# Attention kernel on one core: the part ahead of the loop rebuilt (order of the loads, place of the weight split, banks of the first row maxima)

## What is computed

```
x = x + block(group_norm(x))                   # x: 8 images, 512 channels, 32x32 = 1024 tokens
block(v):
    p    = sigmoid(relu(mean(v) @ w1 + b1) @ w2 + b2)        # gate: one value per channel
    m    = p > 0.5
    hyp  = logmap0(mhsa(expmap0(v * m), hdn weights))        # norms along the 32 pixels of a row
    euc  = mhsa(v * (1 - m), eu weights)
    return hyp + euc
mhsa: q,k,v = split(t @ w_qkv + b_qkv); 8 heads of 64; softmax(q k^T / 8) v; then @ w_o + b_o
```

## Time and profile before

| | us |
|---|---|
| median of 3 runs (4372.26 to 4374.09) | 4373.63 |
| the profiled execution | 4372.58 |
| span of its instructions | 4370.9 |
| of it ahead of the first score of the loop | 209.4 |

### The profile page before, as it was taken

The page is one execution under the profiler, slowest core; times in us unless marked ns, Lnnn a source line. Parts: engine busy times, 40 slices in busy tenths (PEclk is TensorE's granted clock), DMA queues, the critical chain, the costliest instruction groups (busy, mean ns, idle before and its releaser), DMA issues.

```text
span 4370.9 us, 69097 instructions
## 1 busy us (share of the span) xinstructions
PE 4039.6 (92%) x21822; PEld 2426.7 (56%) x21822; DVE 2652.2 (61%) x2771; ACT 1933.8 (44%) x3504; POOL 2668.0 (61%) x1303
## 2 busy tenths in 40 slices
PE   0599989999999989999899998999989998999989
PEld 0355646565465655656465564656546565565645
DVE  4446684557736676465854658455773667646585
ACT  0145453544535445354534545355452544535453
POOL 0167376755758458584676737676575845858467
PEclk9899999999999999999999999999999999999999
DMA  7211212112131211212121121211203121121212
GB/s 273 87 37 49 95 43 95 54 71 73 34 105 44 80 54 56 88 51 87 54 96 41 45 99 39 98 54 61 82 32 108 44 80 54 54 91 51 87 52 83
DMA packets 147413, 314.94 MB, mean 72 GB/s; under 512 B 17600, under 2 KB 30400, under 8 KB 136512
## 3 DMA queue, kind: packets, MB, share of 16 engines
q1 hardware_dynamic: 147008, 309.92, 20.7%
HBM read 259.54 MB, written 50.33 MB: 71 GB/s over the span
## 4 chain that ended last, share of the span: by engine, by line
PE 82%; DVE 9%; issue 4%; DMA 3%; ACT 1%; SPq 0%; DVEq 0%; POOL 0%; ACTq 0%
PE aux_ps L1035 29%; PE acc_ps L1137 20%; PE score_ps L1123 19%; PE aux_ps L1076 8%; PE score_ps L1035 3%; DVE mxp L944 3%; PE aux_ps L1147 2%; DMA xin<-in_x_dram 1%; DMA w_split<-o_t 1%; DVE sc L812 1%; PE aux_ps L1085 1%; DVE sc L819 1%; DVE sc L820 0%; DVE den L972 0%; DVE xin L905 0%
## 5 line engine op out<-in xcount | busy, mean ns | idle before, releaser
L588 POOL TENSOR_TENSOR sums<-sums,probs 128x1024 f32<-128x1024 f32 x768 | 1867.4, 2432 | 892.5 <-ACT probs L714 852.2
L944 DVE TENSOR_REDUCE mxp<-aux_ps 128x2 f32<-128x1024 f32 x1041 | 1274.0, 1224 | 1218.5 <-PE aux_ps L1076 1205.1
L714 ACT ACTIVATE probs<-score_ps 128x512 f32<-128x512 f32 x2048 | 1056.9, 602 | 663.9 <-PE score_ps L1123 656.0
L1137 PE MATMUL acc_ps<-probs,v_y 128*64 128x512 f32 x4096 | 1017.6, 618 | 0.0
L1035 PE MATMUL aux_ps<-xs,w_qk 128*128 128x512 f32 x3168 | 871.0, 414 | 40.8 <-DMA w_qk<-w_split 40.8
L1035 PEld LDWEIGHTS aux_ps<-xs,w_qk 128*128 128x128 f32 x3168 | 572.4, 192 | 465.0 <-issue 301.7
L588 POOL TENSOR_TENSOR sums<-probs 128x1024 f32<-128x1024 f32 x128 | 305.2, 2384 | 538.4 <-ACT probs L714 538.4
L1076 PE MATMUL aux_ps<-k_hi,q_hi 64*128 64x512 f32 x2082 | 481.2, 456 | 159.0 <-DVE mxp L944 153.1
L1137 PEld LDWEIGHTS acc_ps<-probs,v_y 128*64 128x64 f32 x4096 | 251.6, 138 | 477.4 <-issue 438.6
L972 DVE RECIPROCAL den<-den 128x256 f32<-128x256 f32 (+1 forms) x240 | 443.9, 1849 | 7.7 <-ACT den L725 7.7
L1123 PE MATMUL score_ps<-q_hi,k_hi 64*128 64x512 f32 x2048 | 408.8, 395 | 20.6 <-issue 20.6
(11 more groups left out here) (114 smaller groups left out, 3377.9 us busy)
## 6 DMA issues: line engine op xcount, KB each, us to landing
xin<-in_x_dram SPq DMA_DIRECT2D x280, 256.0 KB, 2.9
w_qk<-w_split SPq DMA_DIRECT2D x134, 512.0 KB, 4.1
w_v<-w_split SPq DMA_DIRECT2D x34, 1024.0 KB, 6.8
w_o<-w_split SPq DMA_DIRECT2D x32, 1024.0 KB, 7.1
w_split<-o_t SPq DMA_DIRECT2D x16, 1024.0 KB, 5.5
y<-v_y SPq DMA_DIRECT2D x64, 256.0 KB, 2.0
v_y<-in_x_dram SPq DMA_DIRECT2D x64, 256.0 KB, 2.8
xin<-y SPq DMA_DIRECT2D x64, 256.0 KB, 2.7
```

Of the source, the lines that this page charges most:

```text
L588: pool.tensor_tensor(sums[h][:, :], a, probs[:, g % SLOTS_P, :], ALU.add).then_inc(c_sum[h].sem, 1)
L714: act.activation(probs[:, n % SLOTS_P, token_half(u % 2)], score_ps[:, u % SCORE_BANKS, :], ACT.Exp, scale=SCALE).then_inc(c_exp.sem, 1)
L944: dve.tensor_reduce(mxp[:, :, n, h], ps, AX.X, ALU.max).then_inc(c_free["D"].sem, 1)
L1137: last = nc.tensor.matmul(acc_ps[head(j), :], v_y[:, m, head(2 * p + j)], probs[:, n % SLOTS_P, token_half(j)], start=(m == 0), stop=(m == ...
```

## The change

All of it lies ahead of the loop, apart from waits in the loop for things made there.

- **x once and first.** The 8 chunks of image 0 are loaded once, as SP's first transfers, into the eight parts of `v_y`. Statistics, squares (written to `o_raw`, `squares` and `den`), masks and the operand all work from there. Gate weights and gate biases come next, then six raw weight pieces, then the other biases.
- **The weight split on ACT and POOL.** `split_hi` (ACT, 128x1024 copy) and `split_lo` (POOL, 128x1024 subtraction) replace the two DVE instructions. There are six raw slots (`probs` and `sums`) and ten places for the result (`o_t`, `w_v`, `w_o`, `v_y`). ACT makes three high parts ahead of its two instructions in the gate, three behind them, and the other ten between its read-outs of projection tiles (`SPLIT_BEHIND`). POOL makes three low parts once the gate is done and the other thirteen once the operand is complete. After each low part SP loads the next raw piece and stores the finished one, as before, 16 stores in all.
- **In place.** The projections of pairs 0 and 1 read their weights from the first two split places in `o_t`, and the loop's first v tiles from `w_v`, without a trip to DRAM.
- **The operand's low parts** of image 0 are made by DVE (`x_lo`), between its multiplications.
- **The first row maxima** take three pairs of banks in turn (0 and 1, and the four score banks), the projection tiles bank 2 and the accumulator's bank. The order (`AHEAD`) is: two projection tiles, four maxima, a tile, four maxima, a tile, then four times two maxima and a tile of pair 1.
- In the loop ACT waits for `weights_lo_made` ahead of the first four exponentials of an image and for two stores ahead of its v read-outs; both are met for good once the split is over.

```
+SPLIT_SLOTS = [0, 1, 6, 7, 2, 3, 4, 5, 8, 9, 2, 3, 4, 5, 0, 9]
+SPLIT_FIRST = 6
+SPLIT_BEHIND = {(PAIRS, 0): (6, 7), (PAIRS, 1): (8, 9), (PAIRS, 2): (10, 11), (PAIRS, 3): (12, 13),
+                (PAIRS + 1, 0): (14,), (PAIRS + 1, 1): (15,)}
+LOW_FIRST = 3
+AHEAD = [("qk", PAIRS, 0), ("qk", PAIRS, 1), *[("max", PAIRS, s) for s in range(4)],
+         ("qk", PAIRS, 2), *[("max", PAIRS, s) for s in range(4, 8)], ("qk", PAIRS, 3)]
+for k in range(4):
+    AHEAD += [("max", PAIRS, 8 + 2 * k), ("max", PAIRS, 9 + 2 * k), ("qk", PAIRS + 1, k)]
 def aux_tiles(t):
 
...
-                out += maxima(p, s)
-            out += [((t, "qk", p + 1, k), "Q", (2,))]
+        for what, pp, k in AHEAD:
+            if what == "qk":
+                out += [((t, what, pp, k), "Q", ((2, ACC)[k % 2],))]
+            else:
+                first = (0, FIRST_SCORE, FIRST_SCORE + 2)[k % 3]
+                out += [((t, what, pp, k), "D", (first, first + 1))]
         return out + neg(p) + maxima(p + 1, 0)
     out = []
     for b in range(BATCHES):
...
-        for c, parts in enumerate(SRCS):
-            count[c % 3] += 16 * len(parts)
-            raw_at.append(count[c % 3])
+        raw_at = [16 * sum(len(SRCS[SPLITS[m]]) for m in range(n % RAW_SLOTS, n + 1, RAW_SLOTS)) for n in range(len(SPLITS))]
+        def raw_slot(n):
+            q = n % RAW_SLOTS
+            return probs[:, q, :] if q < SLOTS_P else sums[q - SLOTS_P][:, :]
+        def split_slot(n):
+            q = SPLIT_SLOTS[n]
+            if q < 4:
+                return o_t[:, q // 2, 2 * (q % 2):2 * (q % 2) + 2, :]
+            if q < 8:
+                w = (w_o, w_v)[q // 2 - 2]
+                return w[:, q % 2, :, :, :].rearrange("p a k n -> p a (k n)")
+            return v_y[:, 4 * (q % 2):4 * (q % 2) + 4, :].rearrange("p (a k) n -> p a (k n)", a=2).bitcast(F32R)
 
         def token_half(h):
...
 
         def xin_slot(t, kind, j):
+            if t < 0 and kind == "norm":
+                return (o_raw[:, 0, :], o_raw[:, 1, :], squares[:, :], den[:, 1, :])[j % 4]
+            if t < 0 and kind != "w":
+                return v_y[:, j, :]
             return xin[:, chunk_at(t, kind, j) % XIN, :]
 
         def chunk_in(eng, i, t, kind, j):
 
+            if t < 0 and kind != "w":
+                eng.wait_ge(c_x[j].sem, c_x[j].at(i, 16))
+                return v_y[:, j, :]
...
-                sp.dma_start(bias_o[:, t, :], bo.rearrange("(k p) -> p k", p=P)).then_inc(s_bias, 16)
-            sp.dma_start(bias_1[:, :], b1.rearrange("(p a) -> p a", a=1)).then_inc(s_bias, 16)
-            sp.dma_start(bias_2[:, :], b2.rearrange("(k p) -> p k", p=P)).then_inc(s_bias, 16)
-            def store_split(c):
-                sp.wait_ge(s_split, 2 * c + 2)
-                sp.dma_start(w_split[c], o_t[:, c % 2, 0:2, :].rearrange("p a n -> p (a n)").bitcast(F32)).then_inc(s_wst[c % 2], 16)
...
+            def load_raw(n):
+                raw = raw_slot(n)
+                for src, j in SRCS[SPLITS[n]]:
...
+                    sp.dma_start(dst, src).then_inc(s_raw[n % RAW_SLOTS], 16)
...
-            load_chunks(None, -1, "stats", range(8))
+            for j in range(8):
+                k, cols = x_chunk(j)
+                sp.dma_start(v_y[:, j, :], x_v[0, k, :, cols]).then_inc(c_x[j].sem, 16)
             load_gate(None, -1)
-            load_chunks(None, -1, "norm", range(8))
-            load_chunks(None, -1, "operand", range(8))
+            sp.dma_start(bias_1[:, :], b1.rearrange("(p a) -> p a", a=1)).then_inc(s_gate_bias, 16)
+            sp.dma_start(bias_2[:, :], b2.rearrange("(k p) -> p k", p=P)).then_inc(s_gate_bias, 16)
+            for n in range(RAW_SLOTS):
+                load_raw(n)
+            for t, (bq, bo) in enumerate(((hb_qkv, hb_o), (eb_qkv, eb_o))):
+                for j in range(3):
+                    sp.dma_start(bias_q[:, t, j, :], bq[j * C:(j + 1) * C].rearrange("(k p) -> p k", p=P)).then_inc(s_bias, 16)
+                sp.dma_start(bias_o[:, t, :], bo.rearrange("(k p) -> p k", p=P)).then_inc(s_bias, 16)
+            for n, c in enumerate(SPLITS):
+                sp.wait_ge(s_wlo, n + 1)
+                if n + RAW_SLOTS < len(SPLITS):
+                    load_raw(n + RAW_SLOTS)
+                sp.dma_start(w_split[c].rearrange("p (a n) -> p a n", a=2), split_slot(n).bitcast(F32)).then_inc(s_wst[n], 16)
             for q in s_wst:
-                sp.wait_ge(q, 16 * 8)
+                sp.wait_ge(q, 16)
             i = None
             for j in range(2):
-                load_qk(-1, PAIRS, j)
-            load_wide(w_v, 0, 4, c_wv)
-            for p in (PAIRS + 1, PAIRS + 2):
-                for j in range(2):
-                    load_qk(-1, p, j)
+                load_qk(-1, PAIRS + 2, j)
...
-            for b in range(STEPS_END):
-                x_lo(None, -1, b)
+            def split_lo(n):
+                both = split_slot(n)
+                pool.wait_ge(s_whi, n + 1)
+                pool.tensor_tensor(both[:, 1, :], raw_slot(n), both[:, 0, :].bitcast(F32), ALU.subtract).then_inc(s_wlo, 1)
+            pool.wait_ge(c_keep.sem, c_keep.at(None, 1))
+            for n in range(LOW_FIRST):
+                split_lo(n)
+            pool.wait_ge(c_xlo.sem, c_xlo.at(None, 8))
+            for n in range(LOW_FIRST, len(SPLITS)):
+                split_lo(n)
...
+            def split_hi(n):
+                act.wait_ge(s_raw[n % RAW_SLOTS], raw_at[n])
+                was = [m for m in range(n) if SPLIT_SLOTS[m] == SPLIT_SLOTS[n]]
+                if was:
+                    act.wait_ge(s_wst[was[-1]], 16)
+                if SPLIT_SLOTS[n] == 0 and was:
+                    act.wait_ge(c_aux.sem, c_aux.at(None, at[(-1, "qk", PAIRS, 3)][1] + 1))
+                if SPLIT_SLOTS[n] in (8, 9):
+                    act.wait_ge(c_xlo.sem, c_xlo.at(None, 8))
+                act.activation(split_slot(n)[:, 0, :], raw_slot(n), ACT.Copy).then_inc(s_whi, 1)
+            for n in range(SPLIT_FIRST // 2):
+                split_hi(n)
+            rstd_in(None)
+            for n in range(SPLIT_FIRST // 2, SPLIT_FIRST):
+                split_hi(n)
+            act.wait_ge(c_keep.sem, c_keep.at(None, 1))
+            for j in range(8):
+                square(None, -1, j)
+            clamped(None)
+            for j in range(2):
+                mask(None, -1, OPERAND[j])
+            norm_exp(None)
+            for j in range(2, 8):
+                mask(None, -1, OPERAND[j])
+            for j in range(8):
+                operand_hi(None, -1, j)
+            act.wait_ge(s_bias, 16 * 8)
+            for what, p, k in AHEAD:
+                if what == "qk":
                     qk_hi(None, -1, p, k)
+                    for n in SPLIT_BEHIND.get((p, k), ()):
+                        split_hi(n)
...
+                        if n < SLOTS_P:
+                            act.wait_ge(s_wlo, max(m + 1 for m in range(len(SPLITS)) if m % RAW_SLOTS == n))
...
+                        if t == 0:
+                            act.wait_ge(s_wst[8 if m < 4 else 15], 16)
...
-            for c in range(len(SRCS)):
-                dve.wait_ge(s_raw[c % 3], raw_at[c])
-                if c >= 2:
-                    dve.wait_ge(s_wst[c % 2], 16 * (c // 2))
-                dve.tensor_copy(o_t[:, c % 2, 0, :], probs[:, c % 3, :]).then_inc(s_split, 1)
-                dve.wait_ge(s_split, 2 * c + 1)
-                dve.tensor_tensor(o_t[:, c % 2, 1, :], probs[:, c % 3, :], o_t[:, c % 2, 0, :].bitcast(F32),
-                                  ALU.subtract).then_inc(s_split, 1)
...
+            def x_lo(j):
+                k, cols = x_chunk(j)
+                dve.wait_ge(c_xa.sem, c_xa.at(None, from_scalar_at(-1, "operand", j) + 1))
+                dve.tensor_tensor(xs[:, 1, k, cols], xin_slot(-1, "operand", j), xs[:, 0, k, cols].bitcast(F32),
+                                  ALU.subtract).then_inc(c_xlo.sem, 1)
...
-            for k in range(4):
-                qk_lo(None, -1, PAIRS, k)
-            for k in range(4):
-                for m in range(4 * k, 4 * k + 4):
-                    max_slot(None, -1, PAIRS, m)
-                qk_lo(None, -1, PAIRS + 1, k)
+                if b - 1 in OPERAND:
+                    x_lo(OPERAND.index(b - 1))
+            dve.wait_ge(s_bias, 16 * 8)
+            for what, p, k in AHEAD:
+                if what == "qk":
+                    qk_lo(None, -1, p, k)
+                else:
+                    max_slot(None, -1, p, k)
...
-                    pe.wait_ge(c_wqk[what].sem, c_wqk[what].at(i, 16 * (p - PAIRS + 1 if t < 0 else 4 * t + p - 2)))
+                    if t < 0:
+                        pe.wait_ge(s_wlo, p - PAIRS + 1)
+                    else:
+                        pe.wait_ge(c_wqk[what].sem, c_wqk[what].at(i, 16 * (4 * t + p - 2)))
...
+                def weights(a, c):
+                    if t < 0:
```

(14 more changed lines are left out.)

125 lines of the change are left out of this document (61 added, 64 removed).

## The result

The changed kernel takes **4258.96 us** (median of 4 runs, 4255.99 to 4262.24) against 4373.66 us of the kernel before (4372.26 to 4374.09): a ratio of **0.9738, 95% interval 0.9722 to 0.9755**, 115 us less. The forecast was 4259.0.

A forecast was written before the change was run, and what follows sets the result against it. The loop was taken as PE-bound and unchanged, the prologue as a chain of stages. First score 114.6 us earlier takes the 4370.9 us span to 4256.3; adding 1.7 and 1.05 gives 4259.0 us, range 4250 to 4279.

The forecast's parts named there:

- Step 1: Prologue, loading x: issued first, eight chunks land and their statistics end at 12.4 us, before at 89.3; gain 77 us.
- Step 2: Prologue, gate: ACT's gate instructions wait 4.3 us (0 to 6.5) behind three splits needing raw pieces; squares start at 26.8 us.
- Step 3: Prologue, from squares to the operand's first multiplication: squares and row sum 7.2 us, small steps 8.1 us, ending at 42.1 us.
- Step 4: Prologue, operand on DVE: nine instructions at 0.72 us plus one wait for ACT, so PE starts 7.0 us later, at 49.1.
- Step 5: Prologue, PE's first tile to first score: ACT's last split waits for the seventh load-store pair in the queue; score at 94.8 us.
- Step 6: In the loop: late v read-outs have 20 us of cover and twelve added ACT waits an image are harmless; both cost nothing.
- the queue isn't the limit: Rival, prologue's last stage: loads and stores overlap better, DVE's pace remains; first score at 86.4, time 4250.6 us; chance 0.15.
- (a): Prologue, first tile to first score: DVE's read-outs, 16 maxima and low parts set the length; first score at 86.4 us.
- Half clock throughout: Rival, prologue's projections: PE stays at half clock between waits; first score at 113.2, time 4277.4 us; chance 0.17.
- Late stores: Rival, start of loop: last store lands 40 us in, ACT and PE stop for 10 us; time 4269 us; chance 0.06.
- costly added waits: Rival, loop: twelve added waits in ACT's queue cost PE 15.4 us an image; time about 4382 us; chance 0.01.
- a change that doesn't work: Rival, loop's start still hangs on the stores: first score at about 110, time 4274 us; chance 0.02.

## Why the prediction was right, and where it was not

The total was right to 0.1 us, which is partly luck: the prologue was forecast 2.4 us too short, the profiled loop was 4.5 us shorter than the 4161.5 that I carried over, and the median lay 3.0 us above the profiled execution where I had added 1.05. The three errors nearly cancel. Two executions of the changed kernel had loops of 4157.0 and 4164.1.

- **Step 1, x in (12.4, was 15.03).** The mis-sized term. I took 0.65 us a chunk from the rate of a full queue of mixed loads and stores. With x alone in the queue, the first chunk's statistics start at 6.94 and SP goes on, with all eight landed, at 13.65: 6.7 us for seven chunks, 0.96 each or some 273 GB/s, in place of 4.6 us. That is 2.1 of the 2.6 us, and it isn't the competition behind x. Even the low end, 290 GB/s, was too fast. That the sixteen splits ahead of x were what held this stage is read from the two traces; no run puts them back. The six raw pieces ahead of x, which one run did try, cost the statistics 8.4 us.
- **Step 2, gate (a wait of 4.3, was 4.7).** Right in kind and size, but by two errors: the third raw piece came at 21.8, outside my 16.5 to 21, for the same rate, and the statistics came later too. The 1.06 us of the copy held exactly. Moving the gate instruction ahead of the splits took the whole wait away.
- **Step 3, norms (15.3, was 15.02).** Held. POOL's low parts ran beside the squares (29.77 to 36.74) and cost this path at most 0.4 us: DVE's clamp at its end took 0.61 us where the earlier trace rows has 0.23.
- **Step 4, operand (7.0, was 5.84).** The pace was 0.60 us an instruction, starts of neighbours overlapping their ends, not 0.72. Leaving POOL out of this stretch is what made it so; with POOL it was 8.2.
- **Step 5, the split's queue (45.7, was 46.63).** The mechanism was the one named: the last split waits for the store of n = 9, and the doubled stores moved split and first score by the same 20.3 us. POOL's first low part ended at 57.32 and the last split started 31.75 us later; I had 29.7. Of the 2.1 us between them, 1.4 lie in the last two pairs: 8.86 us from the split at 80.21 to the one at 89.07, against 7.5. The DMA moved 425 GB/s there, which is 3.9 MB where two pairs hold 3.1. The stores of n = 10 and 11, issued from 74.92 on, may be the difference; I had not counted them, and it was not tested.
- **Step 6, nothing given back.** Held, to within the spread of the loop: it was no longer than before, and PE has no gap in its first 38 us.
- **The rivals.** That the queue isn't the limit fell. Where it was taken off the path, by one split to a tile, PE became the limit and not DVE as (a) has it (14.50 and 11.83 us busy of 14.50), and the stage took 40.75 us, not the 37.3 of (a). Half clock throughout did not occur (0.89), but five of the eight tiles took some 3 us and three took 4.0 to 4.5 (the first, which I had at 5.4, and two behind which ACT waited for a store anyway). It was nearer than I knew: with one pair of banks much of it came, at 0.72. My case against it named how the tiles are spread; the banks are what keeps PE from waiting between maxima. Late stores, costly added waits and a change that doesn't work were not seen. (The price of the late stores had a slip: landing 40 us behind the loop's start, where they are needed at 27, makes 13 us, not 10.)

What I missed was a choice, not a number. I read the queue as a limit of the prologue's length. It was one only because of where the splits stood in ACT's stream, two behind one tile and the last ahead of two read-outs; the same sixteen stores, laced more thinly and with the last split behind the read-outs, are hidden.

## What to carry to other kernels

When work that waits for a queue shares an in-order engine with work on the critical path, ask for each wait what stands behind it on that engine; moving the critical instruction ahead (4.7 us here) or spreading the waits (5.9 us) gained time without a byte less in the queue. Give short matmul bursts that are read by a slower engine enough PSUM banks: the wait for the reader was paid, and with it the lower clock of the matmuls around it. Judge a prologue by the time of the loop's first instruction, and the whole by several executions, since the loop of four milliseconds differed by up to 14 us between profiled executions, more than any two of these orders.
